# Bidirectional Mamba block with a ternary projection: who makes the q = 3 input rows, and the order of the front

## The reference

```python
xz = einsum('ed,bld->bel', in_proj_w, xn)            # 512 channels: x and z, 256 each
u = silu(conv4(x) + bias)                            # causal, 4 taps, per channel
delta_low, Bm, Cm = split(x_proj @ u)                # 8 + 16 + 16 rows
delta = softplus(dt_proj @ delta_low + dt_bias)      # 256 channels
dA = exp(delta * A)                                  # 256 channels x 16 states x 512
dBx = delta * u * Bm
h[t] = dA[t] * h[t-1] + dBx[t]                       # the scan
y = (sum over states of h * Cm + D * u) * silu(z)
out = x + (y_fwd + y_bwd) @ out_proj + quant4(xn @ H) @ ternary(w)
```

## Time and profile before

| | us |
|---|---|
| median of 3 runs | 820.13 (819.84 to 820.97) |
| the profiled execution | 819.23 |
| its span, first to last instruction | 817.4 |

### The profile page before, as it was taken

One profiled execution on the slowest core, in us unless ns is written; L12 is line 12 of the kernel. 1 busy time (PEld: TensorE's weight loads), 2 busy tenths in 40 slices (PEclk: granted clock), 3 DMA queues, 4 the chain that ended last, 5 costly groups with the idle time before them and its releaser, 6 DMA issues.

```text
span 817.4 us, 11915 instructions
## 1 busy us (share of the span) xinstructions
PE 726.9 (89%) x3921; PEld 371.3 (45%) x3921; DVE 738.9 (90%) x800; ACT 715.7 (88%) x1358; POOL 726.9 (89%) x355
## 2 busy tenths in 40 slices
PE   7857998899998899989999999988999889999995
PEld 5324344353644436344453536445363444535353
DVE  4648898998999999998999989999999989999996
ACT  3489998999989998999989999799989999899880
POOL 0269989898998989899898989989899998989996
PEclk9889999999999999999999999999999999999699
DMA  6638063160815327080541708143180805417000
GB/s 198 150 66 191 0 146 78 65 132 4 198 34 132 65 69 167 4 192 2 137 99 52 146 4 193 40 121 78 61 174 4 188 6 129 95 45 152 1 20 20
DMA packets 55118, 74.81 MB, mean 92 GB/s; under 512 B 6784, under 2 KB 23568, under 8 KB 55056
## 3 DMA queue, kind: packets, MB, share of 16 engines
q1 hardware_dynamic: 54624, 73.79, 38.5%
q10 hardware_dynamic: 432, 0.26, 0.1%
HBM read 62.49 MB, written 11.53 MB: 91 GB/s over the span
## 4 chain that ended last, share of the span: by engine, by line
PE 41%; ACT 22%; DVE 10%; issue 7%; POOL 3%; DVEq 0%; ACTq 0%
ACT da L407 13%; DVE hst L592 9%; PE y L933 8%; PE b_ps L888 7%; PE pb L814 7%; PE b_ps L910 7%; ACT dbx_t L394 5%; PE y L919 3%; PE pb L823 3%; PE pb L835 3%; POOL hst L695 3%; PE pb L830 1%; ACT x_ln L312 1%; ACT t_exp L336 1%; PE pb L843 1%
## 5 line engine op out<-in xcount | busy, mean ns | idle before, releaser
L695 POOL TENSOR_TENSOR hst<-hst,c_rep 128x1024 f32<-128x1024 f32 x255 | 596.0, 2371 | 43.1 <-DVE hst L592 30.9
L592 DVE TENSOR_TENSOR_SCAN hst<-da,b_ps 128x512 f32<-128x512 f32 x512 | 579.4, 1198 | 20.1 <-issue 13.0
L407 ACT ACTIVATE da<-rep,neg_a 128x511 f32<-128x511 f32 x504 | 330.6, 709 | 10.2 <-DVE hst L592 10.0
L910 PE MATMUL b_ps<-ident,dbx_t 128*128 128x128 f32 x1536 | 225.3, 283 | 53.8 <-DVE hst L592 50.8
L394 ACT ACTIVATE dbx_t<-du_t,b_t 128x256 f32<-128x256 f32 x576 | 248.4, 496 | 4.7 <-PE b_ps L910 3.9
L910 PEld LDWEIGHTS b_ps<-ident,dbx_t 128*128 128x128 f32 x1536 | 170.1, 142 | 162.8 <-DVE hst L592 100.2
L933 PE MATMUL y<-hst,sum_sel 128*32 128x512 f32 x1024 | 137.3, 609 | 0.9 <-POOL hst L695 0.9
L814 PE MATMUL pb<-xnt,conv_wt 128*128 128x512 f32 x240 | 110.5, 603 | 10.9 <-ACT du_t L377 10.1
L705 POOL TENSOR_TENSOR dbx_t<-du_t,b_t 128x1024 f32<-128x1024 f32 x48 | 91.7, 1910 | 13.7 <-ACT du_t L377 13.7
L888 PE MATMUL b_ps<-du,spread_sel 32*128 32x512 f32 x256 | 89.2, 669 | 1.8 <-POOL du L760 1.2
L581 DVE TENSOR_TENSOR b_ps<-b_ps,b_rep 128x1024 f32<-128x1024 f32 x64 | 77.8, 1217 | 7.9 <-PE b_ps L888 6.6
(11 more groups left out here) (119 smaller groups left out, 460.4 us busy)
## 6 DMA issues: line engine op xcount, KB each, us to landing
rep<-d_scr SPq DMA_DIRECT2D x128, 256.0 KB, 9.2
c_rep<-bc_scr SPq DMA_DIRECT2D x64, 256.0 KB, 4.9
d_scr<-t_pos SPq DMA_DIRECT2D x16, 512.0 KB, 3.0
b_rep<-bc_scr SPq DMA_DIRECT2D x64, 64.0 KB, 2.2
x_ln<-x SPq DMA_DIRECT2D x8, 256.0 KB, 3.9
x_res<-x SPq DMA_DIRECT2D x8, 256.0 KB, 2.8
out<-x_res SPq DMA_DIRECT2D x8, 256.0 KB, 2.3
rep<-x SPq DMA_DIRECT2D x7, 256.0 KB, 4.4
```

Source lines behind the costliest of these rows:

```text
L407: nc.scalar.activation(da[s % 2][:, j, 1:L], rep[d][h][:, j, 1:L], ACT.Exp, scale=neg_a[:, d, h, j, q:q + 1]).then_inc(decay_done, 1)
L592: nc.vector.tensor_tensor_scan(hst[s % RING][:, j, :], da[s % 2][:, j, :], b_ps[:, j, :], 0.0, ALU.mult, ALU.add).then_inc(scan_done, 1)
L695: nc.gpsimd.tensor_tensor(hst[s % RING][:, two, :], hst[s % RING][:, two, :], c_rep[d][:, q:q + 1, :].broadcast_to([P, 2, L]), ALU.mult).t ...
L910: ins = tr(b_ps[:, j, P * c:P * (c + 1)], dbx_t[(NX * d + q - 1) % 2][:, c, NJ * h + j, :, :].rearrange("p r e -> p (r e)"), ident[:, :])
```

## The change

ACT makes all four rows of q = 3 (4 more activations of 128x256 a unit, one for each chunk c), and POOL's product of q = 3 goes; the counts of `bm_pool` follow. In the front, ACT runs a softplus of one column ahead of its wait for the step projections; POOL's `moments` go behind the two products delta*u; the second convolution goes from between the spreads to behind the copies of slot 1, and its `u_sigmoid` and `make_u` go into slots 0 and 1 of the first unit; slot 2's transposes go ahead of the first unit's step projections, with chunk 0 of q = 2 made in slot 2 instead of slot 1.

```diff
 keep_bt, keep_dut (ACT):
-                wait(act, bm_pool, NX * (V - 1))
+                wait(act, bm_pool, (NX - 1) * (V - 1))
 def first_softplus():
+                nc.scalar.activation(fcol[:, 0:1], const[:, 0:1], ACT.Softplus)
                 act.wait_ge(u_ready, 2)
 def inputs_t(d, U, q, c) (ACT):
-                for r in ACT_R:
+                for r in range(NR) if q == NX else ACT_R:
 ACT, front and unit:
             keep_dut(0, 0, 1)
-            u_sigmoid(1, 1, 0)
-            u_sigmoid(1, 1, 1)
             inputs_t(0, 0, 1, 0)
...
                     if s == 0:
-                        if nxt and V > 1:
+                        if nxt:
                             u_sigmoid(e, V, 0)
...
                         inputs_t(d, U, 1, 3)
-                        if nxt and V > 1:
+                        if nxt:
                             u_sigmoid(e, V, 1)
                     if s == 2:
+                        if U == 0:
+                            inputs_t(d, U, 2, 0)
                         inputs_t(d, U, 2, 1)
...
-                    if s == 1:
+                    if s == 1 and U > 0:
                         inputs_t(d, U, 2, 0)
 DVE, unit:
+                    if s == 1 and V == 1:
+                        make_u(e, V, 0)
                     scan(b, d, s, 1)
-                    if s == 0 and V == 1:
-                        make_u(e, V, 0)
+                    if s == 1 and V == 1:
                         make_u(e, V, 1)
 POOL:
-            moments(slice(NC, NB * NC))
             pool.wait_ge(first_delta, 1)
             pool.wait_ge(fwt_filled, 1)
             ... (du[:, 0], du[:, 1])
+            moments(slice(NC, NB * NC))
...
                     if s == 3:
                         if nxt:
                             make_du(e, V)
-                        inputs_free(U, 3)
-                        inputs_t(d, 3)
 PE, inputs():
-                    pe.wait_ge(bm_pool, NX * (2 * b + d) + q)
+                    pe.wait_ge(bm_pool, (NX - 1) * (2 * b + d) + min(q, NX - 1))
 PE, front:
             copies(0, 0, 1)
-            conv(1, 1, 0, range(2, TAPS), weights_ready, 2)
-            step_replicas(1, (0, 1))
-            conv(1, 1, 1, range(2), weights_ready, 2)
-            step_replicas(1, (2, 3))
-            conv(1, 1, 1, range(2, TAPS), weights_ready, 2)
+            step_replicas(1, range(NJ))
             du_transposed(0, 0, decay_done, 2 * NJ)
 PE, unit:
-                    next_inputs(s, 0)
+                    if s != 1 or U > 0:
+                        next_inputs(s, 0)
                     if s == 0 and U == 0:
-                        next_inputs(s, 1)
+                        next_inputs(0, 1)
+                        conv(1, 1, 0, range(2, TAPS), weights_ready, 2)
+                        conv(1, 1, 1, range(TAPS), weights_ready, 2)
                     if s == 0 and nxt:
                         x_proj(e, V)
...
-                    if s > 0 or U > 0:
+                    if s > 1 or U > 0:
                         next_inputs(s, 1)
+                    if s == 0 and U == 0:
+                        next_inputs(1, 0)
+                        next_inputs(1, 1)
                     if s == 0 and nxt:
                         steps(e, 1, xdbl_ready, V + 1)
                         steps(e, 0, xdbl_ready, V + 1)
```

## The result

The changed kernel took 815.86 us (median of 5 runs, 815.67 to 816.80) against 820.13 us before (819.82 to 820.97): a ratio of 0.9944, 95% interval 0.9931 to 0.9958. It is faster, by 4.3 us in the medians. The forecast was 815.8.

What follows compares the result with a forecast made beforehand. Four engines were nearly full, none the bound by load alone, so waits were priced place by place. Front -5.9 and rows +1.6 gave -4.3: 819.23 to 814.9 us profiled, plus 0.9 to the median, 815.8; range 812.0 to 820.2.

Steps and rivals of the forecast that it cites:

- Part 1: Rows of q = 3 moved from POOL to ACT, summed over all batches and the end: +1.6 us.
- Batch 0: First batch: forward unit pays the full +1.6 us without idle time; backward unit saves 1.9 of its scale wait.
- Forward units of batches 1 to 6: ACT's activations before `keep_bt` nearly hidden by idle time, those after delay the next convolution: +0.85 us each.
- Backward units: Batches 1 to 6: ACT's additions hidden by idle time, DVE's wait for POOL's scale goes: -0.40 us each.
- The end: Last unit: POOL, relieved of one product, stops being last ahead of DVE's `y_gated`: -0.8 us.
- Part 2: The front's reordering: slot 3's first exponentials start earlier on ACT and the gain carries through: -5.9 us.
- Last exponential of `first_decays`: Front, spreads without the convolution between them: ends at 36.2 us instead of 41.9, 5.7 earlier.
- From `du_t` to slot 3: Front stretch up to slot 3's exponentials: keeps its 19.1 us, no new waits, 1.0 for step projections.
- A: Rival: the front runs at full clock; front -8.3, sum -6.7, 813.4 us; chance 0.15.
- B: Rival: front's clock stays half into the convolution, ACT waits; front -3.6, sum -2.0, 818.1 us; chance 0.18.
- C: Rival: ACT's added rows covered nowhere, each unit paying 1.62 us; +16, 832 us; chance 0.07.
- D: Rival: forward units pay all of ACT's added 1.62 us; +4.6, sum +0.3, 820.4 us; chance 0.10.

Runs made afterwards that it cites:

- the rows alone: The kernel before with only the fourth row of q = 3 moved to ScalarE, its front unchanged: 821.19 us, ratio 1.0008.
- The front alone: The changed kernel with POOL making the fourth row of q = 3 as before, so only the front's moves remain: 816.29 us, ratio 0.9949.
- the rows backward: The changed kernel with ScalarE making the fourth row of q = 3 in backward units only, POOL in forward units: 809.38 us, ratio 0.9866.
- the two traces compared above: Changed kernel with step projections ahead of slot 2's transposes (816.99 us); backward-only ScalarE fourth row, POOL making rows 2 and 3 forward (805.84 us).

## Why the prediction was right

**Part 1 (forecast +1.6; the trace has +0.7).** Each mechanism showed where it was placed.
- Batch 0, forward: forecast +1.6, measured +1.59 (-4.23 at slot 3's exponentials, -2.64 at the convolution), and the same with the rows alone. The front alone loses 0.54 of it by itself, so with the front in place the rows added 1.05. Backward: -1.9, measured -1.85.
- Forward units of batches 1 to 6: forecast +0.85 each, measured +0.8 (39.34 us between the two convolutions around one of them, 425.46 to 464.80; 38.52 before, 428.84 to 467.36). Hidden before `keep_bt`, paid after it: the two kernels with the row in one direction only confirm both halves.
- Backward units: forecast -0.40, the wait in the earlier trace rows, measured -0.50 where undisturbed, -2.75 for six. The wait was the right term and slightly too small: the scale's reciprocal, now not waited for, also took 0.15 in place of 0.18 us; the rest is not traced.
- The end: forecast -0.8, measured -1.04. POOL is no longer last, as forecast.
So part 1 was 0.9 too pessimistic, from the last three.

**Part 2 (forecast -5.9; the trace has -4.2).** This is the term that was mis-sized, by 1.7, in the three steps of its chain:
- Last exponential of `first_decays`: forecast 36.2, measured 36.72. Of three rounds one ran at full clock (1.89 us) and two at half (2.85); the forecast's two prices, 1.76 and 2.9, were nearly right, and it took a value between.
- `du_t`: forecast 2.0 later, measured 2.7 later (39.44). The step that failed: the forecast let the clock be back by then. It stayed at half to 40 us, so the eight transposes took 1.94 us, against 1.04 before.
- From `du_t` to slot 3: forecast 19.1, measured 19.54, with a wait of 0.64 for the convolution that the forecast said would not be there. It comes from the copies of slot 1, still at half clock: 1.77 us against 1.14. The wait for the step projections was 0.69, where the forecast had 1.0. The DMAs of slot 2 made no wait, as forecast.

With part 2 too optimistic by 1.7 and part 1 too pessimistic by 0.9, the sum was off by only 0.8, and the offset from span to median hid that.

**The rivals.** A (full clock) did not come: 0.50 in 30 to 40 us. Its -8.3 doesn't follow from the steps either, an end at 34.1 in place of 36.2 gives -8.0. B (half clock into the convolution) came in part. Its sign showed, ACT idle before a `u_sigmoid`, but in this trace the clock was back when the convolution began at 40.44, and its twelve matmuls ran at full (5.42 us). In others with the same front the convolution did begin at half, and ACT waited longer: 1.42 us with the front alone, 1.17 with the rows backward. The forecast's price for B was not worked out right: half 0 ready at 43.4, with ACT there at 40.6, is a wait of 2.8 and a front of -3.1, not -3.6. The measured -4.2 lies between B and the forecast. C (no cover anywhere) is out: `keep_bt` no longer waits, and the backward unit got shorter. D would have made forward units +1.62; they are at +0.80. The period is 95.94, against 96.1 forecast. What I missed altogether is that the moved convolution also fills PE's idle time ahead of x_proj and of the step projections: before, the latter ran at half clock after 6.11 us of idle time, 3.78 us; after, they took 1.88.

**The rule weighed.** The changed trace has the load at 23.30 for 1.28 us and the next activation at 24.59. The drain that the Trainium skill ("ScalarE: Activation LUTs", "What ACT_TABLE_LOAD costs") adds behind a load is not there either; to go by the row was right. Its rule on the clock ("TensorE: Matmul & The Clock Gate", "What you observe") has the clock rise after sustained matmul activity. This trace doesn't agree in 30 to 35 us: PE was busy 4.98 of 5.00 us by its records and granted half, and it stayed at half to 40.

**A better version.** The kernel with four ScalarE rows backward and two forward takes 805.84 us, 1.8% under before, and beats the change as a whole by about 10 us. Putting the step projections first in it may be worth another 0.8, an estimate from the two traces compared above; that was not run.

## What to carry to other kernels

When work moves between two nearly full engines, price it unit by unit: the same edit paid 0.5 us in one kind of unit and cost 0.8 in the other, and splitting it by direction was worth more than the whole change. A block moved out of a start-up chain can count twice, for the delay it leaves and for the gap it fills; look at what stands idle where it goes. Compare medians and profiled executions separately: a sum can be 0.8 us off and still land on the median. And before a difference of 1 us between two traces is put down to an edit, look whether a stretch that the edit doesn't touch differs too, here the period of a middle batch and the clock of the front.

## What the runs showed of the hardware

- TensorE at full occupancy by the records can be granted half clock: 4.98 of 5.00 us busy with 32-row matmuls, at 0.50. Wide matmuls ahead of that stretch did not prevent the fall; single groups of them within it went, in the one trace, with a clock of 1.00 up to 44.5 us.
- The same idle time can cost the clock or not: after 2.42 us without work for PE, x_proj took 1.99 us in one trace and 3.52 and 3.56 in two others.
- The same batches took 96.00 to 96.03 us in the three traces of one chip and 95.94 in others.
- The clock made a small delay larger: 0.66 us on ScalarE at 28 us became 1.45 at 39.
- Where PE finished earlier it idled longer (4.60 us against 2.67) and lost the clock again: 3.78 us for x_proj against 1.98.
